# Attention and mixture-of-experts layer on one core: first head's maxima made beside the q and k products, v kept in memory

## The chip, the cores and the metric

The kernel runs on one core of a Trainium2 chip. Its engines are PE (matrix products), DVE, ACT and POOL (element work), SP (here only an issuer of DMAs) and 16 DMA engines. The metric is the time of one execution in device microseconds (us), smaller is better.

## The reference, cut to what matters

Input x has 4 batches of 2048 tokens of 256 values. The layer norm of x goes both to an attention of 16 heads of 16 values and to a mixture of 16 experts; the sum of x and both results is returned.

```python
xn = _layernorm(x)
q = (xn @ Wq.T + bq).reshape(b, s, HEADS, HEAD_DIM) * SCALE      # k, v alike, without the scale
scores = jnp.einsum('bqhd,bkhd->bhqk', q, k)
probs = jax.nn.softmax(scores, axis=-1)
out = jnp.einsum('bhqk,bkhd->bqhd', probs, v).reshape(b, s, d) @ Wo.T + bo
# experts: two of 16 are gated per token, each expert takes its 1024 best tokens of a batch, gelu(x w1) w2, layer norm
```

## The kernel before

The kernel has four stages, each a block of per-engine programs; an engine enters a stage when all engines have left the one before.

**norm** (L157 to L343) goes over 16 blocks of 512 tokens (4 a batch). DVE makes statistics (L226, L230) and normalised tokens (L239), PE transposes them (L320) and multiplies with Wv and the gate's weights (L330), DVE's `take` adds the bias and writes v into `v_all` (L246), 64 KB in each partition that stay on chip. SP loads x two blocks ahead (L198) and stores the normalised tokens (L202). DVE's order is `take` of turn t - 1, `scale` of block t + 2, `statistics` of block t + 3.

**project** (L346 to L484): for each of 16 blocks four products of 128x512 (two halves each of q and k, L385). ACT evacuates each twice (L409, L411), POOL subtracts to get the rounding rest (L424), SP stores both parts, 512 KB a product (L432). One buffer for each of the four: ACT writes part m of a block only when part m of the block before has landed, and PE makes product m of a block only when ACT has written part m of the block before. Beside this DVE makes the experts' routing (L447 to L482); PE waits for it after 4 blocks (L392), transposes the routes, and goes on.

**attend** (L487 to L875) has 64 heads. A head n has a first pass, 32 pairs of products (L771, 48 rows) whose maxima DVE takes (L852); from them the shift is made (ACT L731, POOL L579, DVE's transpose L843) and put by four small DMAs into two rows of q's features (`put_shift`, L653). Then come the scores (L781, 50 rows), their exponentials (ACT L724) and the weighing with v (L790), by key tile of 128. The first pass of the following heads is written between the scores: during head g PE makes the last 22 pairs of head g + 1 and the first 10 (`EARLY`) of head g + 2. Only head 0's 32 pairs and head 1's first 10 stand ahead of all scores (L820 to L825). A `feed` (L641) is four DMAs from `q_parts` and `k_parts`: two of 256 KB, which write 32 rows of 8 KB from a source of shape [2, 16, 2048], and two of 128 KB over 16 rows; each head needs one for the first pass (LOWER) and one for the scores (UPPER). SP issues all of them, in order. POOL copies each head's v from `v_all` to `v_head` (L573), and looks for the experts' bounds.

**finish** makes the experts, the output projection and the sum.

## Time and profile before

| | us |
|---|---|
| median of 3 runs (lowest to highest) | 3443.64 (3443.12 to 3445.09) |
| the profiled execution | 3444.21 |
| its span in the trace | 3442.4 |
| norm stage, from the start to the first product of q and k | 102.2 |
| project stage, to the first feed's issue | 239.4 |
| first passes ahead of the scores, to the first score | 315.8 |
| PE busy over the span | 3296.2 (96%) |
| DVE busy | 2894.2 (84%) |
| ACT busy | 2526.4 (73%) |

Times of instructions are counted from the span's start. A line in a profile row (L771) is the line of the kernel before. "x8" is the number of instructions in a row; "[12.29 <-DVE cand L482]" says that the engine stood 12.29 us before it, until that instruction. PEclk is the clock granted to PE: 1.00 is 2.4 GHz, 0.50 is 1.2 GHz. A DMA share is the mean busy share of the 16 DMA engines.

### The profile page before, as it was taken

The numbers are of one execution on the slowest core, as the hardware profiler recorded it, in microseconds if no ns is written. First come the engines' busy times: TensorE is split into PE (matmuls) and PEld (weight loads), VectorE is DVE, ScalarE is ACT, GpSimd is POOL, SyncE is SP. The second block draws the span as 40 slices with busy tenths as digits, with TensorE's granted clock in tenths as the row PEclk, the third lists the DMA queues.
The fourth block names the chain that finished last, engine by engine and source line by source line (L and its number), as shares of the span: only waits on it lengthen the run. The fifth ranks groups of instructions, "written<-read, shape, count | busy, mean of one in ns | idle before, by whom it ended". The sixth has DMA issues, their size and how long they took to land. (4 is left out here: it accounts for less than half of the span.)

```text
span 3442.4 us, 74610 instructions
## 1 busy us (share of the span) xinstructions
PE 3296.2 (96%) x20848; PEld 1706.4 (50%) x20848; DVE 2894.2 (84%) x2987; ACT 2526.4 (73%) x5726; POOL 929.1 (27%) x1339
## 2 busy tenths in 40 slices
PE   7868999999999999999999999999999999599998
PEld 6424444444444444444444444444444444288887
DVE  7508999999999999999999999999999998267777
ACT  3452888888888888888888888888888888443433
POOL 2550222222222222222222222222222222144443
PEclk9986999999999999999999999999999999799999
DMA  6581111122111211111121111211111121355553
GB/s 198 173 241 33 50 54 54 54 60 59 58 56 55 56 56 55 54 54 54 54 60 56 56 55 54 63 56 56 55 54 54 54 59 47 112 136 169 160 164 117
DMA packets 133063, 272.29 MB, mean 79 GB/s; under 512 B 22512, under 2 KB 68656, under 8 KB 120432
## 3 DMA queue, kind: packets, MB, share of 16 engines
q1 hardware_dynamic: 130464, 266.68, 26.7%
q8 instruction: 176, 2.88, 0.4%
q10 hardware_dynamic: 2256, 1.36, 0.2%
q14 instruction: 167, 1.37, 0.1%
HBM read 173.59 MB, written 84.93 MB: 75 GB/s over the span
## 5 line engine op out<-in xcount | busy, mean ns | idle before, releaser
L852 DVE TENSOR_REDUCE half_max<-m_ps 128x1 f32<-128x1024 f32 x2048 | 2413.4, 1220 | 324.5 <-PE m_ps L771 308.8
L724 ACT ACTIVATE prob<-s_ps 128x512 f32<-128x512 f32 (+1 forms) x5120 | 2188.3, 520 | 425.8 <-PE s_ps L781 423.2
L781 PE MATMUL s_ps<-q_feat,k_feat 50*128 50x512 f32 (+1 forms) x5120 | 1538.0, 396 | 7.5 <-issue 4.7
L771 PE MATMUL m_ps<-k_feat,q_feat 48*128 48x512 f32 x4096 | 1405.1, 448 | 55.9 <-DMA k_feat<-k_parts 28.4
L781 PEld LDWEIGHTS s_ps<-q_feat,k_feat 50*128 50x128 f32 x5120 | 796.2, 184 | 983.3 <-ACT prob L724 870.6
L790 PE MATMUL a_ps<-prob,v_head 128*32 128x512 f32 x8192 | 1091.6, 605 | 0.0
L771 PEld LDWEIGHTS m_ps<-k_feat,q_feat 48*128 48x128 f32 x4096 | 616.3, 187 | 287.5 <-DVE half_max L852 248.6
L579 POOL TENSOR_TENSOR shift<-row_max,shift 128x16 fp32r<-128x16 f32 x64 | 14.2, 222 | 1213.0 <-ACT shift L731 1213.0
L790 PEld LDWEIGHTS a_ps<-prob,v_head 128*32 128x32 f32 x8192 | 161.2, 108 | 253.7 <-issue 211.7
L1134 ACT ACTIVATE g_hi<-g 128x512 fp32r<-128x512 f32 x128 | 81.0, 632 | 243.8 <-DVE g L1172 199.8
L1297 POOL TENSOR_TENSOR g_lo<-g,g_hi 128x512 fp32r<-128x512 f32 x128 | 173.0, 1352 | 229.2 <-ACT g_hi L1134 229.2
L606 POOL TENSOR_SCALAR step_of<-route,cand 64x256 f32<-64x256 f32 x217 | 198.6, 915 | 44.5 <-POOL held L607 38.3
L573 POOL COPY v_head<-v_all 128x256 f32 (+1 forms) x64 | 25.3, 397 | 660.2 <-PE a_ps L790 660.1
L607 POOL TENSOR_TENSOR held<-held,step_of 64x256 f32<-64x256 f32 x217 | 157.6, 726 | 39.8 <-POOL step_of L606 39.8
L1172 DVE TENSOR_TENSOR g<-g,mask_bc 128x512 f32<-128x512 f32 x128 | 133.5, 1043 | 36.0 <-ACT g L1131 30.7
L1067 PE MATMUL o_ps<-w_hi,g_hi 128*128 128x256 f32 x512 | 144.6, 282 | 6.1 <-issue 3.7
L1067 PE MATMUL o_ps<-w_lo,g_hi 128*128 128x256 f32 x512 | 144.3, 282 | 0.0
L1067 PE MATMUL o_ps<-w_hi,g_lo 128*128 128x256 f32 x512 | 143.1, 280 | 0.0
L1056 PE MATMUL h_ps<-xn_hi,w_hi 128*128 128x512 f32 x256 | 105.7, 413 | 32.0 <-DMA b_rows<-b_parts 32.0
L1131 ACT ACTIVATE g<-h_ps,b_col 128x512 f32<-128x512 f32 x128 | 86.2, 674 | 25.7 <-PE h_ps L1056 25.7
L1067 PEld LDWEIGHTS o_ps<-w_hi,g_hi 128*128 128x128 f32 x512 | 96.5, 189 | 12.0 <-issue 7.1
L1056 PE MATMUL h_ps<-xn_lo,w_hi 128*128 128x512 f32 x256 | 102.1, 399 | 0.0
(132 smaller groups left out, 1904.1 us busy)
## 6 DMA issues: line engine op xcount, KB each, us to landing
q_feat<-q_parts SPq DMA_DIRECT2D x128, 256.0 KB
k_feat<-k_parts SPq DMA_DIRECT2D x128, 256.0 KB
q_parts<-parts SPq DMA_DIRECT2D x32, 512.0 KB, 4.8
k_parts<-parts SPq DMA_DIRECT2D x32, 512.0 KB, 4.8
q_feat<-q_parts SPq DMA_DIRECT2D x128, 128.0 KB
k_feat<-k_parts SPq DMA_DIRECT2D x128, 128.0 KB
att_dram<-att SPq DMA_DIRECT2D x64, 256.0 KB, 14.0
mask_bc<-mask_b SPq DMA_DIRECT2D x128, 128.0 KB, 4.4
```

The lines of the kernel that those rows point to most:

```text
L606: do(pool.tensor_scalar(step_of[:, :], t["route"][:, c * PART:(c + 1) * PART], bound, None, ALU.is_ge))
L607: do(pool.tensor_tensor(held[:, :], held[:, :], step_of[:, :], ALU.add))
L724: act.activation(prob[tile(r, kt) % R][:, cols(j)], s_ps[slot(r, kt, j) % R][:, wide(j)], ACT.Exp).then_inc(exped, 1)
L771: ins = pe.matmul(m_ps[p % 2][:, k * BLK:(k + 1) * BLK], q_feat[r % 2][LOW, qt * P:(qt + 1) * P], k_feat[r % 2][LOW, key:key + BLK], start ...
L781: pe.matmul(s_ps[slot(r, kt, j) % R][:, wide(j)], k_feat[r % 2][UP, kt * P:(kt + 1) * P], q_feat[r % 2][UP, cols(j)], start=True, stop=Tru ...
L790: ins = pe.matmul(a_ps[qb * VW:(qb + 1) * VW, :], v_head[r % R][:, kt, :], prob[tile(r, kt) % R][:, qb * BLK:(qb + 1) * BLK], start=(kt == ...
L852: dve.tensor_reduce(half_max[r][:, p // 2, p % 2:p % 2 + 1], m_ps[p % 2][:, :], AX.X, ALU.max).then_inc(maxed, 1)
L1056: ins = pe.matmul(h_ps[e % 2][:, :], w, v, start=(c == 0 and k == 0), stop=(c == KC - 1 and k == 2))
L1067: ins = pe.matmul(o_ps[k], v, w[:, e, :], start=(e == 0 and m == 0), stop=False)
L1131: act.activation(g[e % 2][:, :], h_ps[e % 2][:, :], ACT.Gelu, bias=b1_col[:, e:e + 1]).then_inc(gelu, 1)
L1172: dve.tensor_tensor(g[e % 2][:, :], g[e % 2][:, :], mask_bc[q % 2][:, e % QTR, :], ALU.mult).then_inc(gated, 1)
L1297: pool.tensor_tensor(g_lo[e % 2][:, :], g[e % 2][:, :], g_hi[e % 2][:, :].bitcast(F32), ALU.subtract).then_inc(split, 1)
```

## The change

v goes to memory: `v_all` is replaced by `v_buf`, two batches long, from which SP stores each batch (2.10 MB) in the norm stage; before each block of DVE's `take` stands a wait for the store two batches back. In the attention SP loads each head's v (128 KB) and POOL copies from there. The maxima's tiles, the features and their semaphores are made before the project stage; the two banks of maxima (`m_ps`) also take the transposed routes. In the project stage PE waits for the routing after 6 blocks instead of 4, and of the remaining 40 products each is followed by one pair of first passes, two of them by two: all 32 pairs of head 0 and the first 10 of head 1. SP issues three feeds (heads 0 and 1 for the first pass, head 0 for the scores) once batch 0's parts have landed, behind the fifth block's stores and ahead of the sixth's. The shift of head 0 is made and put at the end of the stage. The ones in the features are written by two POOL memsets at the start instead of POOL and ACT at the start of the attention. The mask's steps get memory of their own instead of `v_all`'s.

The diff, cut to its core:

```diff
+PAIRS = ST * 2
+EARLY = 10
+LOADS = 4
+BEFORE = 6
 HALVES = NBLK * KC
...
 
-            for u in range(2):
-                load(u, u)
-            with sp.Fori(1, NBLK // 2) as i:
-                for u in range(2):
-                    load(i * 2 + u, u)
-                    store(i * 2 + u - 2, u)
-            for u in range(2):
-                store(NBLK - 2 + u, u)
+            def store_v(b):
+                sp.wait_ge(taken, TPB + (b + 1) * ST)
+                sp.dma_start(t["v_dram"][b * H:(b + 1) * H].rearrange("h p f -> p h f"),
+                             v_buf[:, b % 2, :, :, :].rearrange("p h s d -> p h (s d)")).then_inc(v_stored, 16)
+
+            sp.sem_inc(v_stored, 32)
+            for blk in range(2):
+                load(blk, blk)
+            for blk in range(2, NBLK):
+                if blk % BPS == 0 and blk >= 2 * BPS:
+                    store_v(blk // BPS - 2)
+                load(blk, blk % 2)
+                store(blk - 2, blk % 2)
+            store_v(B - 2)
+            for blk in range(NBLK - 2, NBLK):
+                store(blk, blk % 2)
+            store_v(B - 1)
+            sp.wait_ge(v_stored, 32 + 16 * B)
             for u in range(2):
                 sp.wait_ge(xn_stored[u], 16 * (NBLK // 2))
 
...
+                dve.wait_ge(v_stored, (blk // BPS) * 16 + 16)
                 for k in range(TPB):
                     dve.wait_ge(projected, blk * TPB + k + 1 + 2 * TPB)
                     dve.tensor_tensor(
-                        v_view[:, ds(blk // BPS, 1), ds((blk % BPS) * TPB + k, 1), :, :].rearrange("p b s h d -> p (b s h) d"),
+                        v_view[:, ds((blk // BPS) % 2, 1), ds((blk % BPS) * TPB + k, 1), :, :].rearrange("p b s h d -> p (b s h) d"),
                         vg_ps[:, k, 0:D].rearrange("p (h d) -> p h d", h=H),
                         t["bv_bc"][:, :].rearrange("p (h d) -> p h d", h=H), ALU.add).then_inc(taken, 1)
...
+            pool.wait_ge(ident_made, 1)
+            for u in range(2):
+                pool.memset(t["k_feat"][u][96:P, :].bitcast(F32), 1.0).then_inc(cleared, 1)
+                pool.wait_ge(cleared, 3 + u)
...
-            def chunks(lo, hi):
-                with pe.Fori(lo, hi) as blk:
-                    for m in range(M):
-                        pe.wait_ge(rounded, blk * M + m + 1)
-                        for c in range(KC):
-                            half = m % KC
-                            ins = pe.matmul(qk_ps[m][:, :], weights[m][:, c, half * P:(half + 1) * P],
-                                            t["tok_all"][:, ds(blk, 1), c * BLK:(c + 1) * BLK].rearrange("p n s -> p (n s)"),
-                                            start=(c == 0), stop=(c == KC - 1))
-                        ins.then_inc(scored, 1)
-
-            chunks(0, NBLK // 4)
+            def chunk(blk, m):
+                pe.wait_ge(rounded, blk * M + m + 1)
+                for c in range(KC):
+                    half = m % KC
+                    ins = pe.matmul(qk_ps[m][:, :], weights[m][:, c, half * P:(half + 1) * P],
+                                    t["tok_all"][:, ds(blk, 1), c * BLK:(c + 1) * BLK].rearrange("p n s -> p (n s)"),
+                                    start=(c == 0), stop=(c == KC - 1))
+                ins.then_inc(scored, 1)
+
+            def first_pass(n, p):
+                if p == 0:
+                    pe.wait_ge(fed_low[n], 16 * LOADS)
+                pe.wait_ge(maxed, n * PAIRS + p + 1)
+                qt, half = divmod(p, 2)
+                for k in range(2):
+                    key = half * 2 * BLK + k * BLK
+                    ins = pe.matmul(m_ps[p % 2][:, k * BLK:(k + 1) * BLK], q_feat[n][low, qt * P:(qt + 1) * P],
+                                    k_feat[n][low, key:key + BLK], start=True, stop=True)
+                ins.then_inc(piece, 1)
+
+            with pe.Fori(0, BEFORE) as blk:
+                for m in range(M):
+                    chunk(blk, m)
 
             pe.wait_ge(routed, 1)
             for s in range(ST):
-                ins = pe.transpose(route_ps[:, s * P:(s + 1) * P], tmp[:, s * B:(s + 1) * B, :].rearrange("p b e -> p (b e)"),
-                                   t["ident"][:, :])
+                half, at = divmod(s, ST // 2)
+                ins = pe.transpose(m_ps[half][0:B * E, at * P:(at + 1) * P],
+                                   tmp[:, s * B:(s + 1) * B, :].rearrange("p b e -> p (b e)"), t["ident"][:, :])
             ins.then_inc(route_t, 1)
-            chunks(NBLK // 4, NBLK)
+
+            early = PAIRS + EARLY
+            turns = (NBLK - BEFORE) * M
+            for blk in range(BEFORE, NBLK):
+                for m in range(M):
+                    chunk(blk, m)
+                    at = (blk - BEFORE) * M + m
+                    for p in range(at * early // turns, (at + 1) * early // turns):
+                        first_pass(p // PAIRS, p % PAIRS)
...
+            act.wait_ge(row_maxed, 1)
+            act.activation(shift[:, 0, :], row_max[0][:, :], ACT.Copy).then_inc(shift_rounded, 1)
 
...
+            pool.wait_ge(shift_rounded, 1)
+            pool.tensor_tensor(shift[:, 1, :], row_max[0][:, :], shift[:, 0, :].bitcast(F32), ALU.subtract).then_inc(shift_done, 1)
...
-            with sp.Fori(0, NBLK) as blk:
-                for m in range(M):
-                    sp.wait_ge(split, blk * M + m + 1 + M)
-                    store(blk, m)
+            def feed(n, where, done):
+                q, k = (t[w][:, n * HD:(n + 1) * HD, :] for w in ("q_parts", "k_parts"))
+                pair, single = slice(where, where + 2 * HD), slice(where + 2 * HD, where + FEAT)
+                sp.dma_start(q_feat[n][pair, :].bitcast(F32), q).then_inc(done[n], 16)
+                sp.dma_start(k_feat[n][pair, :].bitcast(F32), k[0:1].broadcast_to([2, HD, S])).then_inc(done[n], 16)
+                sp.dma_start(q_feat[n][single, :].bitcast(F32), q[0:1].rearrange("k d s -> (k d) s")).then_inc(done[n], 16)
+                sp.dma_start(k_feat[n][single, :].bitcast(F32), k[1:2].rearrange("k d s -> (k d) s")).then_inc(done[n], 16)
+
+            def stores(lo, hi):
+                with sp.Fori(lo, hi) as blk:
+                    for m in range(M):
+                        sp.wait_ge(split, blk * M + m + 1 + M)
+                        store(blk, m)
+
+            stores(0, BPS + 1)
+            for m in range(M):
+                sp.wait_ge(stored[m], 16 * BPS + 16)
+            for n in range(2):
+                feed(n, LOWER, fed_low)
+            feed(0, UPPER, fed_up)
+            stores(BPS + 1, NBLK)
+            sp.wait_ge(shift_turned, 1)
+            rows = q_feat[0][UPPER + FEAT:UPPER + FEAT + SHIFT, :].bitcast(F32).rearrange("k (q j p) -> k q j p", j=quarters, q=ST)
+            for j in range(quarters):
+                sp.dma_start(rows[:, :, j, :], turned[j * SHIFT * ST:(j + 1) * SHIFT * ST, :]).then_inc(shift_in, 16)
             for m in range(M):
                 sp.wait_ge(stored[m], 16 * NBLK + 16)
 
...
-            do(dve.tensor_copy(t["route"][:, :], route_ps[:, :]))
+            for half in range(2):
+                do(dve.tensor_copy(t["route"][:, half * 2 * BLK:(half + 1) * 2 * BLK], m_ps[half][0:B * E, :]))
+            dve.sem_inc(maxed, 2)
+            for p in range(PAIRS):
+                dve.wait_ge(piece, p + 1)
+                dve.tensor_reduce(half_max[0][:, p // 2, p % 2:p % 2 + 1], m_ps[p % 2][:, :], AX.X, ALU.max).then_inc(maxed, 1)
+            dve.wait_ge(maxed, PAIRS + 2)
+            dve.tensor_reduce(row_max[0][:, :], half_max[0][:, :, :], AX.X, ALU.max, negate=True).then_inc(row_maxed, 1)
+            for p in range(EARLY):
+                dve.wait_ge(piece, PAIRS + p + 1)
+                dve.tensor_reduce(half_max[1][:, p // 2, p % 2:p % 2 + 1], m_ps[p % 2][:, :], AX.X, ALU.max).then_inc(maxed, 1)
+            dve.wait_ge(shift_done, 1)
+            dve.transpose(turned[:, :], shift[:, :, :].rearrange("p k q -> p (k q)").bitcast(F32)).then_inc(shift_turned, 1)
 
...
-            def copy_v(n, r):
-                pool.tensor_copy(v_head[r][:, :, 0:HD],
-                                 t["v_all"][:, :, :, :, :].rearrange("p b h s d -> p (b h) s d")[:, ds(n, 1)].rearrange("p n s d -> p (n s) d")
-                                 ).then_inc(v_ready, 1)
+            pool.wait_ge(ones_set, R)
+
+            def copy_v(r, turn):
+                wait_apart(pool, v_loaded[r], (turn + 1) * 16, t["passed"][2])
+                pool.tensor_copy(v_head[r][:, :, 0:HD], v_in[r][:, :, :]).then_inc(v_ready, 1)
...
+            def load_v(n, r):
+                sp.dma_start(v_in[r % R][:, :, :].rearrange("p s d -> p (s d)"),
+                             t["v_dram"][ds(n, 1)].rearrange("n p f -> (n p) f")).then_inc(v_loaded[r % R], 16)
+
             sp.sem_inc(att_out, 16)
             sp.sem_inc(prepared_out, 16)
-            for n in range(2):
-                feed(n, n, LOWER, fed_low)
+            for n in range(R):
+                load_v(n, n)
+            sp.wait_ge(piece, PAIRS)
+            feed(2, 0, LOWER, fed_low)
             for dst, src in ((shift_bc[:, :], "beta"), (staged[:, 0:D].bitcast(F32), "bo")):
                 sp.dma_start(dst, t[src].partition_broadcast(P)).then_inc(bias_in, 16)
-            sp.wait_ge(ones_made, 2)
-            feed(0, 0, UPPER, fed_up)
...
                 if following:
                     put_shift(g + 1, (r + 1) % 2)
                 if third:
+                    sp.wait_ge(v_ready, g + 1)
+                    load_v(g + 3, r)
...
-            for p in range(PAIRS):
-                for k in range(2):
-                    pass1(0, 0, 0, p, k)
-            for p in range(EARLY):
-                for k in range(2):
-                    pass1(1, 0, 1, p, k)
```

## Rows read from the trace of the kernel before

**Rows 1.** Busy us by stretch: span, then PE, PEld, DVE, ACT, POOL; PEclk, DMA share, GB/s.

```profile
20.00:100.00 80.00, 73.45 (x361) 59.59 (x360) 64.84 (x237) 28.91 (x56) 16.40 (x26) 1.00 0.51 174
...
142.00:148.00 6.00, 5.78 (x19) 3.88 (x20) 2.23 (x3) 0.00 (x0) 0.00 (x0) 0.50 0.00 0
...
152.00:232.00 80.00, 77.52 (x181) 34.01 (x179) 0.00 (x0) 58.21 (x91) 58.00 (x46) 1.00 1.00 293
...
260.00:300.00 40.00, 36.77 (x63) 15.87 (x64) 37.31 (x34) 0.21 (x1) 0.72 (x1) 0.50 0.08 28
```

**Rows 2.** Timeline of PE and of SP's queue, 225 to 316: start, us, what.

```profile
225.92 3.60 PE L385 MATMUL qk_ps<-tok_all,wkT_sb 128*128 x8
...
239.36 0.84 SPq L644 DMA_DIRECT2D q_feat<-q_parts  x1
...
257.87 2.07 PE L771 MATMUL m_ps<-k_feat,q_feat 48*128 48x512 f32 x4 [28.35 <-DMA k_feat<-k_parts]
...
298.25 0.65 SPq L644 DMA_DIRECT2D q_feat<-q_parts  x1
...
301.09 3.97 SPq L653 DMA_DIRECT2D q_feat<-turned  x4
...
315.78 0.76 PE L781 MATMUL s_ps<-q_feat,k_feat 50*128 50x512 f32 x1 [4.75 <-issue]
```

**Rows 3.** Groups of instructions, 0 to 340: DVE's reduces (busy, mean ns | idle).

```profile
L852 DVE TENSOR_REDUCE half_max<-m_ps 128x1 f32<-128x1024 f32 x59 | 70.0, 1220 | 122.0 <-PE m_ps L771 121.6
```

**Rows 4.** Timeline of PE in the attention: the weighing products, one key tile apart.

```profile
338.88 1.06 PE L790 MATMUL a_ps<-prob,v_head 128*32 128x512 f32 x8
...
341.42 1.07 PE L790 MATMUL a_ps<-prob,v_head 128*32 128x512 f32 x8
```

**Rows 5.** DMA queues, 3425 to 3443: GB/s in slices of 0.45 us; issue and landing.

```profile
GB/s 0 18 0 0 0 0 36 0 0 0 0 0 0 0 0 0 0 18 0 0 0 0 0 0 0 0 0 0 0 0 0 0 0 280 344 348 194 0 0 0
...
out<-res SPq DMA_DIRECT2D x1, 512.0 KB, 2.9
```

**Rows 6.** DMA queues, 152 to 230, the products stage: packets.

```profile
DMA packets 11917, 22.99 MB, mean 295 GB/s; under 512 B 695, under 2 KB 695, under 8 KB 11917
```

**Rows 7.** Timeline of DVE and SP, 40 to 48, the norm stage.

```profile
40.35 0.21 DVE L250 TENSOR_TENSOR logits<-vg_ps,bg_bc 128x64 f32 x1
...
42.26 0.38 SPq L198 DMA_DIRECT2D x_in<-in_x  x1
...
47.41 1.40 DVE L226 BATCH_NORM_STATS2 bn<-x_in 128x6 f32<-128x256 f32 x4
```

**Rows 8.** DMA issues of the whole run: KB each, median us to landing.

```profile
x_in<-in_x SPq DMA_DIRECT2D x16, 512.0 KB, 4.0
...
tok_hi_dram<-staged SPq DMA_DIRECT2D x32, 256.0 KB, 13.0
```

**Rows 9.** Timeline of PE at the start of the products stage.

```profile
102.20 3.69 PE L385 MATMUL qk_ps<-tok_all,wqT_sb 128*128 x8 [1.27 <-ACTq L401]
...
119.47 3.60 PE L385 MATMUL qk_ps<-tok_all,wkT_sb 128*128 x8
...
122.90 3.60 PE L385 MATMUL qk_ps<-tok_all,wqT_sb 128*128 x8
```

**Rows 10.** Timeline, 121 to 146: POOL, SP's queue and PE around the routing.

```profile
121.45 15.45 POOL L424 TENSOR_TENSOR parts<-f32s,parts 128x512 fp32r<-128x512 f32 x8 [0.26 <-ACT parts L411]
...
134.72 2.58 SPq L432 DMA_DIRECT2D k_parts<-parts  x2
...
142.22 3.62 PE L394 MATMUL route_ps<-ident,work 128*64 128x128 f32 x16 [12.29 <-DVE cand L482]
```

**Rows 11.** DMA queues, 250 to 254, 266 to 270, 278 to 282 (tenths, 0.1 us each).

```profile
DMA packets 28, 0.21 MB, mean 53 GB/s; under 512 B 2, under 2 KB 2, under 8 KB 2
...
DMA packets 60, 0.18 MB, mean 45 GB/s; under 512 B 10, under 2 KB 42, under 8 KB 42
...
DMA  0300300300400400000000000000000000000000
```

101 lines of the change are left out of this document (49 added, 52 removed).

## The prediction

> **What bounds the kernel now.** I read the page's forty slices first: PE is busy in nearly all of them, except the start and one slice before the last stage. Of the start I then read the table by stretch [rows 1]. The norm stage keeps PE and DVE near full (73 and 65 of 80 us). In the products stage PE and the DMA engines are both full: from 152 to 232 PE is busy 77.5 of 80 and the DMA share is 1.00, at 293 GB/s. Between the stages PE stands: 229.5 to 257.9 [rows 2], 28.4 us, while stores land and the first feeds travel. Then come 32 pairs of first passes for head 0 and 10 for head 1, paced by DVE's reduce (1.22 us each [rows 3], with its wait 1.27: 41 and 13 us), with the clock at 0.50 and only DVE and PE at work [rows 1]. The first score starts at 315.8 [rows 2]. From there each key tile takes 2.55 us of PE without a break [rows 4], up to the end of the attention. So what the change is worth is read from one number: **when the first score starts**. All that is saved or lost before it moves the end one to one, if the steady state is untouched.
>
> The sum is made against the profiled run, 3444.2 us (span 3442.4), which lies 0.6 us above the median of 3443.6.
>
> **Part 1, v through memory: what the norm stage pays.** Removed: nothing, since `take` still writes the same tile of the same size. Added: four stores of 2.10 MB each, in pieces of 1 KB. The nearest row is the output store at the kernel's end, also 1 KB pieces: 344 GB/s in its burst and 2.9 us to landing for 0.5 MB [rows 5]. I take 300 GB/s, so 7.0 us a store. Bounds: 6.1 us at 344 GB/s; and 13.4 us, if each of 2048 packets costs an engine what a packet of the products stage does (16 engines x 78 us / 11917 = 0.105 us, and 128 packets an engine) [rows 6].
> - Two of the stores stand in SP's queue ahead of the loads of blocks 8 and 12. The store may start once DVE has taken the batch's last tile (40.6), the load is issued at 42.3 and its statistics start at 47.4 [rows 7]. The load lands a median 4.0 us after issue [rows 8], so it has 1.1 us to spare. With some 0.9 us from issue to the first byte, the store's data move from about 41.4 to 48.4, where the load's began at 43.2: 5.2 us later, less 1.1 of slack, less 0.7 of waits that DVE regains: 3.4 us, twice, 7 us. Lower bound 0, if the load overtakes; upper 10 each, with the slow store. Behind DVE stand PE and ACT, which have no second source of work.
> - The third store is behind nothing that is waited for. The fourth is issued after the very last `take` (about 101.5), and the stage's end waits for it; before, PE stood only 1.3 us between the stages [rows 9]. Issue 0.4, data 7.0, landing 1.6: **9 us** (8 to 16).
> Together +16 us (+8 to +36). The DMA page of the Trainium skill (DMA: Bandwidth & Descriptors, Anatomy of one DMA) fits a transfer as about 2.0 us plus bytes at 436 GB/s, for a store 6.8 us from issue to landing where I use 9; by it this part would be some +10. The bursts of the output store stay below that rate, so my own number stands. POOL's two memsets run while the first x load travels (4.0 us from issue to landing [rows 8]) and are priced at nothing; at 1.3 us each, a POOL operation of 128x512 [rows 1], they would cost at most 3 us if that cover were gone. The copies of v into v_head are as many and as large as before.
>
> **Part 2, products up to the feeds.** Before, PE stood 12.3 us for `routed`, up to 142.2, and nothing was stored then [rows 10]. With 6 blocks ahead of that wait instead of 4 the wait is gone; this is worth up to 12 us and is inside the sum below. PE starts at half clock after about 10 us of standing, as it did at 142 [rows 1]; I add 1.5 us. The fourth block's last store was issued at about 137.3; while DVE's routing chain runs, POOL takes 15.45 us for 8 subtractions, so a block takes 7.7 [rows 10]. The fifth block is stored at 145, and with parts 1 and 2 the feeds are issued at 145 + 16 + 1.5 = **162.5**.
>
> **Part 3, the feeds inside the products.** Twelve DMAs, three feeds. Before, they were issued from 239.4; PE had the first at 257.9, after 18.5 us [rows 2], and the last of them moved at 279.5 [rows 11], 40 us after the first issue. In between the rate was 53 GB/s, in packets of 8 KB [rows 11], where 16 engines moved 293 and were full [rows 1]. I read this as two engines at 26 GB/s each. These are the 256 KB DMAs, whose source has an outermost size of 2. The other engines stood; 32 packets of 512 B to 2 KB, left of the two bias loads that were issued behind the first two feeds, moved only at 266 to 270 [rows 11], and in the attention, where feeds are always about, a 256 KB store takes 13 us to land [rows 8]. So the order on those two engines is kept, and whatever is issued later waits for them. A split of parts needs all 16 engines, so block 5's stores land only when the three feeds have drained: 40.1 us, less 4 for the two bias loads that now come later (an estimate, 32 packets in the stretch 266 to 270), plus 1.5 of stores still ahead, 37.6; plus 1.8 (0.5 MB at 293 GB/s) and 1.6 to landing: 41 us after issue, **203.5**. ACT cannot write block 6's parts before that (a landed store is its wait), and PE's product (7, 0) waits for ACT. Before it, PE has only block 6 and the passes 0 to 3 between, which need the first feed at about 182. So PE mostly stands from 164 to 204.5.
> The Trainium skill (same page, Rules for kernel authors) says that an outermost size c below 16 confines a DMA to at most c engines. The trace agrees. Its specification of some 27 GiB/s an engine would drain 1.57 MB over two engines in 27 us rather than 36; the sum would come out 9 us lower by it. I keep the measured drain.
>
> **Part 4, products and passes to the end.** From 204.5: 36 products at 1.72 us (8 records in 3.43 us from start to start, four records a product [rows 9]) make 62; 38 pairs of passes at 0.43 us make 16 (at half clock four passes run 0.43 us apart [rows 2], so 0.21 at full). PE is thus the slower side at 8.6 us a block, against 7.2 for the stores. Half clock after the stall costs 3.2 us, as after 142 (some 6.4 us at 0.50) [rows 1]. End of the last product: about 285. DVE has 42 reduces of 1.22 us, 51 us, beside 80: hidden. Without that cover they would be the 54 us that stand there now.
> Then 1.3 us ACT (two operations, 58.2 us for 91 [rows 1]), 1.3 POOL (58.0 for 46), 0.5 for shift and transpose (an estimate, tiles of 128x32), 4.0 for four put DMAs [rows 2], 1.6 to landing: first score at **293.7**. The 10 us that it waited before for these puts, which stood behind the third feed's pair DMAs (issued at 298.2, puts to 305.1, score 315.8 [rows 2]), are gone, since that feed now comes later. The first weighing needs v in SBUF two key tiles later, 5 us at least, and three 128 KB loads come first in SP's queue: hidden. Its cover is only these 5 us; a late load would show there.
>
> **Sum.** 315.8 - 293.7 = 22 us earlier. 3444.2 - 22 = **3422 us**. What moves it: v stores 8 less or 20 more (that end is a rival below), the drain by 5 either way. Its own range is 3408 to 3437.
>
> **Part 5, the steady state.** Each head gains one SP issue (about 0.4 us) and one wait that is long met; it stands before a feed that has a whole head (41 us) of time. POOL's copy gets a wait on a load issued a head earlier. I price both at nothing; covers are those 41 us. The mask's steps get their own memory, which changes no instruction.
>
> **Rivals.**
> - *The feeds hold up less* (chance 0.18). If stores overtake the feeds on the two engines, these still carry 37.6 us of feeds plus 11 blocks at 7.2, from 162.5: 279. First score not before 285, gain 31, 3413. If other engines take a share, PE alone bounds: 163 + 69 + 18 + 2 + 8 = 260, gain 55, 3389. For it: the share is low only while nothing else is in the queue. Against: the bias packets.
> - *v stores run at the packet price of the products stage* (0.12): part 1 is 36 instead of 16; 3442, no change. For it: pieces are 1 KB and strided by 128 KB. Against: the output store.
> - *The clock stays low* (0.08), the rival on the other side. Place: products and passes after the stall. Price: at 1.2 GHz 78 us of PE work become 156, 3501, slower. It decides from 42 us spent at half clock. For it: from 260 to 300 PE was busy 92% and the clock stayed at 0.50 [rows 1], with these same 48-row passes. Against: the transposes and products after 142 brought it back in 6.4 us. By the Trainium skill (TensorE: Matmul & The Clock Gate, Part 1) sustained activity releases the throttle, which would leave my forecast as it is; rows 260 to 300 show that these passes alone did not.
> - *A small loss in each head* (0.08) from the extra load before the feed: 0.3 us x 64 = 19 us gives 3442, 0.5 us gives 3455. Nothing in the rows shows SP or DMA late there.
> - *The change does not do what it says*, passes only after the products: excluded by the written order, but a stall of `maxed` or of feed 1 would look like it; it is inside the forecast's range.
>
> **Numbers.** Forecast 0.54. A measurement of this kernel can tell 0.2%, 7 us, so faster means below 3437. Faster: 0.50 of the forecast, 0.18, 0.02 of the rest: 0.70. Same: 0.04 + 0.08 + 0.04 = 0.16. Slower: 0.04 + 0.08 + 0.02 = 0.14. Range 3393 to 3448: from near the first rival's far end to beyond the slow stores.
>
> **What would show it.** DVE standing before the statistics of blocks 8 and 12, some 3 us each; a 10 us gap before the first product; no gap before the route's transposes; a stretch of some 40 us in the products stage with 53 GB/s while ACT waits for a stored part; PE then busy to about 285; the first score near 294; 2.55 us a key tile as before. Wrong would be: a full DMA share through the feeds, a clock of 0.50 late in the stage, or a head longer than before.

## The result, and the profile after

The changed kernel takes **3462.3 us** (median of 5 runs, 3460.1 to 3465.7) where the kernel before takes 3444.0 beside it (5 runs, 3443.1 to 3445.1): a ratio of 1.0054, 95% interval 1.0040 to 1.0069. It is 18 us slower, outside the range of the forecast. The profiled execution took 3464.7, its span is 3462.9; before it was 3444.2 and 3442.4.

| stage mark, us from the start | before | forecast | after |
|---|---|---|---|
| first product of q and k | 102.2 | 118 | 120.5 |
| first feed issued | 239.4 | 162.5 | 162.7 |
| product (7, 0) | | 204.5 | 205.0 |
| end of the last product of q and k | 229.5 | 285 | 299.4 |
| first score | 315.8 | 293.7 | 306.7 |
| last transpose of a shift | 2910.7 | 2888.7 | 2908.6 |
| last output of a head taken | 2961.3 | 2939.3 | 2978.4 |
| first h_ps product of the last stage | 2993.3 | 2971.3 | 3007.5 |
| end of the span | 3442.4 | 3420.4 | 3462.9 |

(The last four marks of the forecast are those of before, less 22.) First the page of after, the engines' busy time and the granted clock in 40 slices:

```profile
PE 3326.3 (96%) x20848; PEld 1710.0 (49%) x20848; DVE 2900.9 (84%) x2988; ACT 2525.8 (73%) x5724; POOL 933.5 (27%) x1340
PEclk9988999999999999999999999999999999699999
```

and of the page of before its clock:

```profile
PEclk9986999999999999999999999999999999799999
```

PE is busy 30 us longer with as many instructions. One digit of the clock near the start is higher than before (8 for 6), one near the end lower (6 for 7), so the clock is no worse at the start, and what it costs must lie late. The timeline of PE, norm and products stage of after [rows 2, 9 for before]:

```profile
120.47 2.07 PE L424 MATMUL qk_ps<-tok_all,wqT_sb 128*128 x2 [9.45 <-ACTq L462]
...
181.60 1.22 PE L436 MATMUL m_ps<-k_feat,q_feat 48*128 48x512 f32 x2 [13.08 <-DMA k_feat<-k_parts]
...
204.96 3.78 PE L424 MATMUL qk_ps<-tok_all,wqT_sb 128*128 128x512 f32 x4 [10.11 <-ACT parts L472]
...
216.49 0.73 PE L436 MATMUL m_ps<-k_feat,q_feat 48*128 48x512 f32 x2
217.15 1.98 PE L424 MATMUL qk_ps<-tok_all,wqT_sb 128*128 128x512 f32 x4
219.06 0.73 PE L436 MATMUL m_ps<-k_feat,q_feat 48*128 48x512 f32 x2
219.72 1.98 PE L424 MATMUL qk_ps<-tok_all,wqT_sb 128*128 128x512 f32 x4
...
297.40 1.98 PE L424 MATMUL qk_ps<-tok_all,wkT_sb 128*128 128x512 f32 x4
...
306.71 0.76 PE L862 MATMUL s_ps<-q_feat,k_feat 50*128 50x512 f32 x1 [6.18 <-DMA q_feat<-turned]
```

Up to product (7, 0) all came as forecast: 9.45 us of waiting at the stage's end, the first pass at 181.6, the hold until 205. ACT's longest wait there is for a stored part:

```profile
ACT parts L472 <- DMA q_parts<-parts: 35.6, 2, 35.0
```

(us in total, times, longest). Then one turn, a product and a pair of passes, takes 2.57 us (217.15 to 219.72) where I had 1.72 + 0.43 = 2.15. So the first score comes 9.1 us earlier than before, not 22. The rest was lost later, where I had put nothing. ACT in the last head, after, and PE at the pause:

```profile
2924.09 1.64 ACT L806 ACTIVATE prob<-s_ps 128x256 f32<-128x256 f32 x4 [0.42 <-PE s_ps L862]
2927.21 2.82 ACT L806 ACTIVATE prob<-s_ps 128x512 f32<-128x512 f32 x6 [1.49 <-PE s_ps L862]
2930.87 2.35 ACT L806 ACTIVATE prob<-s_ps 128x256 f32<-128x256 f32 x5 [0.84 <-PE s_ps L862]
2934.94 2.35 ACT L806 ACTIVATE prob<-s_ps 128x256 f32<-128x256 f32 x5 [1.71 <-PE s_ps L862]
...
2978.39 0.60 ACT L818 ACTIVATE att<-a_ps 128x512 f32<-128x512 f32 x1 [2.13 <-PE a_ps L871]
```

```profile
2927.86 1.04 PE L862 MATMUL s_ps<-q_feat,k_feat 50*128 50x512 f32 x3 [1.15 <-ACT prob L806]
```

and the table by stretch of the same time, after and then before (columns: stretch, length, busy us of PE, its weight loads, DVE, ACT and POOL with counts; granted clock, DMA share, GB/s):

```profile
2905.00:2920.00 15.00, 14.24 (x82) 5.53 (x78) 11.48 (x10) 12.56 (x32) 7.50 (x4) 1.00 0.06 20
2930.00:2950.00 20.00, 20.00 (x69) 7.35 (x65) 0.00 (x0) 11.59 (x26) 0.00 (x0) 0.50 0.08 20
2955.00:2960.00 5.00, 5.00 (x17) 2.06 (x16) 0.00 (x0) 2.97 (x7) 0.00 (x0) 0.50 0.00 0
```

```profile
2930.00:2950.00 20.00, 19.02 (x104) 7.35 (x104) 0.00 (x0) 16.65 (x40) 1.28 (x1) 1.00 0.10 28
2955.00:2960.00 5.00, 4.88 (x33) 1.68 (x32) 0.00 (x0) 4.16 (x10) 0.00 (x0) 1.00 0.00 0
```

There is a pause of 1.49 us on ACT (on PE 1.15) in the last head, and behind it the clock is 0.50 from 2929.3 to 2977.1, nearly to the end of the attention: a key tile takes 4.07 us instead of 2.55 (2934.94 less 2930.87), since PE is now the slower side at 100% busy. From the last transpose of a shift to the last output it is 69.8 us after and 50.6 before: **19.2 us lost in one head**.

The 42.5 us between the forecast's end (3420.4) and the span's are thus: 13.0 at the first score, 7.9 in the first heads, 1.0 gained in the heads behind them, 19.2 in the last head, 2.9 gained up to the first h_ps product, 6.3 in the last stage (455.4 us instead of 449.1). The 7.9 are 4.9 up to the third transpose of a shift (at 390.3, only 4.2 us ahead of before's 394.5) and 3.0 up to the next (434.4 against 435.6), while the clock was 0.50 from 386.4 to 396.7; at the fifth after is 1.1 us ahead (475.6, before 476.7), at the last 2.1.

In the first heads and in the last stage two stalls of DVE are new. After:

```profile
382.06 0.19 DVE L927 TENSOR_REDUCE row_max<-half_max 128x16 f32<-128x32 f32 x1
383.60 3.49 DVE L925 TENSOR_REDUCE half_max<-m_ps 128x1 f32<-128x1024 f32 x3 [1.36 <-PE m_ps L852]
...
3043.72 0.74 DVE L1250 TENSOR_TENSOR z<-z,o_ps 128x256 f32<-128x256 f32 x2
3049.80 0.75 DVE L1250 TENSOR_TENSOR z<-z,o_ps 128x256 f32<-128x256 f32 x2 [5.34 <-issue]
```

The first is named a wait for PE, but PE itself stood 1.57 us there for DVE; the second lies between two of four equal additions, and PE, whose products they take, stood 3.2 us there for DVE too. Before, the first gap is 0.24 us and the four additions run through:

```profile
388.43 1.23 DVE L852 TENSOR_REDUCE half_max<-m_ps 128x1 f32<-128x1024 f32 x1 [0.24 <-issue]
...
3029.60 1.40 DVE L1178 TENSOR_TENSOR z<-z,o_ps 128x256 f32<-128x256 f32 x4
```

A third new pause is ACT's, nine times, once a turn of its loop over six heads, some 6.5 us behind a transpose and 0.8 to 1.1 us long; a head with it takes 41.5 to 41.8 us instead of 41.1. One of the nine:

```profile
1390.75 1.57 ACT L806 ACTIVATE prob<-s_ps 128x512 f32<-128x512 f32 x3 [1.02 <-PE s_ps L862]
```

### The profile page after: what moved, and what is told of

Same layout as the page of the kernel before. It is cut to its first block and busy times, and to the rows that moved or that the text cites. A ratio compares the mean times of both kernels' runs of the same rounds, so it can differ in the third digit from the quotient of the medians.

```text
span 3462.9 us, 74796 instructions
## 1 busy us (share of the span) xinstructions
PE 3326.3 (96%) x20848; PEld 1710.0 (49%) x20848; DVE 2900.9 (84%) x2988; ACT 2525.8 (73%) x5724; POOL 933.5 (27%) x1340
## 3 DMA queue, kind: packets, MB, share of 16 engines
q10 hardware_dynamic: 2256, 1.36, 0.2%
## 5 line engine op out<-in xcount | busy, mean ns | idle before, releaser
L925 DVE TENSOR_REDUCE half_max<-m_ps 128x1 f32<-128x1024 f32 x2006 | 2363.4, 1220 | 218.2 <-PE m_ps L852 209.3
L852 PE MATMUL m_ps<-k_feat,q_feat 48*128 48x512 f32 x4012 | 1357.7, 443 | 18.4 <-DVE half_max L925 18.2
L871 PE MATMUL a_ps<-prob,v_head 128*32 128x512 f32 x8192 | 1105.9, 612 | 0.0
L852 PEld LDWEIGHTS m_ps<-k_feat,q_feat 48*128 48x128 f32 x4012 | 598.5, 186 | 218.2 <-DVE half_max L925 208.8
L871 PEld LDWEIGHTS a_ps<-prob,v_head 128*32 128x32 f32 x8192 | 162.0, 108 | 262.5 <-issue 213.9
L658 POOL COPY v_head<-v_in 128x256 f32<-128x256 f32 x64 | 25.5, 398 | 676.5 <-PE a_ps L871 675.1
L487 POOL TENSOR_TENSOR parts<-f32s,parts 128x512 fp32r<-128x512 f32 x64 | 89.1, 1401 | 92.5 <-ACT parts L472 92.4
```

The source lines that it names most:

```text
L487: pool.tensor_tensor(parts[m][:, 1, :], f32s[m][:, :], parts[m][:, 0, :].bitcast(F32), ALU.subtract).then_inc(split, 1)
L852: ins = pe.matmul(m_ps[p % 2][:, k * BLK:(k + 1) * BLK], q_feat[r % 2][LOW, qt * P:(qt + 1) * P], k_feat[r % 2][LOW, key:key + BLK], start ...
L871: ins = pe.matmul(a_ps[qb * VW:(qb + 1) * VW, :], v_head[r % R][:, kt, :], prob[tile(r, kt) % R][:, qb * BLK:(qb + 1) * BLK], start=(kt == ...
L925: dve.tensor_reduce(half_max[r][:, p // 2, p % 2:p % 2 + 1], m_ps[p % 2][:, :], AX.X, ALU.max).then_inc(maxed, 1)
```

## The experiments

Two theories of the late losses went into them. **A:** the pauses are an engine's waits for its own next instructions, at fixed places of its code, which the change has moved; a pause lets the clock fall, and in the last head, without first passes between, it stays low. **The rivals:** the v loads or later transfers cost it; or it is chance of timing. For the early loss: changing between products and passes costs PE 0.43 us a turn, or the passes are dearer there. Ratios are to the kernel before, run beside each (3444.1 to 3445.2).

**e1, passes up to the end.** Edit, in PE's `step` of the attention (`idle_pass` is one product of head 63's first pass into `m_ps`, whose result nobody reads; only the first of them waits, for the last maxima):

```diff
+                    if isinstance(g, int) and g >= HEADS - 2 and (g == HEADS - 1 or kt >= 12):
+                        return lambda j: idle_pass(g, r, kt, k, j)
```

> The changed kernel, with first passes whose results nobody reads added to the end of head 62 and to head 63, where it has none (their output is left unread, the result is unchanged). Theory A (the clock): the 19 us that the last head loses come from one pause of 1.2 to 1.5 us at 2927, after which the clock falls to 0.50 and PE, with scores and weighing alone, never gets it back. In heads 0 to 2, where passes stand between, it came back after such a pause within some 13 us. Then the clock returns here too, the attention ends near 2965 instead of 2978, and the whole takes 3447 to 3453. Rival B (work per key tile): the clock stays at 0.50 whatever PE does; a key tile with four passes more then takes 5.1 us instead of 4.07, twelve of them some 12 us more, 3470 to 3478. Rival C: the pause itself comes from a late transfer or an engine and goes or stays by chance; then nothing is added in a key tile (2.55 us) and the pause is seen at another place or not at all, 3444 to 3462.

Measured 3446.0 (3441.6 to 3450.4, 10 runs; ratio 1.0004, 0.9995 to 1.0014), 16 us less than the changed kernel. ACT in the last head:

```profile
2928.20 2.82 ACT L806 ACTIVATE prob<-s_ps 128x512 f32<-128x512 f32 x6 [1.98 <-PE s_ps L870]
2932.61 1.31 ACT L806 ACTIVATE prob<-s_ps 128x256 f32<-128x256 f32 x3 [1.58 <-PE s_ps L870]
...
2936.56 2.13 ACT L806 ACTIVATE prob<-s_ps 128x256 f32<-128x256 f32 x5 [1.36 <-PE s_ps L870]
...
2964.33 0.60 ACT L818 ACTIVATE att<-a_ps 128x512 f32<-128x512 f32 x1 [1.58 <-PE a_ps L879]
```

The pause is in the same place and no shorter; the clock is back at 2936.3, after 6.9 us at 0.50, where 47.8 us of scores and weighing had not brought it back. The last output comes at 2964.3 instead of 2978.4, and the last head takes 55.2 us, before 50.6. So the pause costs little and the clock behind it much. The Trainium skill (TensorE: Matmul & The Clock Gate, What's actually happening) has sustained activity release the throttle; the changed kernel's last head does not agree, busy 20.00 of 20 us at 0.50, and a caveat of the same page (Seeing it yourself), that the gate has been seen stuck for over 50 us, at K = 1/4 where here it is 0.50, comes nearer.

**e2, passes by twos.**

```diff
-                    for p in range(at * early // turns, (at + 1) * early // turns):
-                        first_pass(p // PAIRS, p % PAIRS)
+                    if at % 2 == 1:
+                        for p in range((at - 1) * early // turns, (at + 1) * early // turns):
+                            first_pass(p // PAIRS, p % PAIRS)
```

> The changed kernel with two pairs of first passes after every second product of q and k, instead of one after each: as many products and passes, half the changes from one kind to the other. Theory A (a change from product to pass and back costs PE about 0.43 us, since the first matmul after it starts together with its weight load): the 19 changes saved are worth 8 us, the last product starts near 289 instead of 297.4, the first score near 298.5 instead of 306.7. Rival B (the passes themselves are dearer beside products, through the DMA share or the 48 rows): nothing changes, 297 and 307. Rival C (passes in twos wait for DVE's reduces of 1.22 us, two buffers): the last product is later, by up to 19 x 1.2 us. The whole: 3454, 3462 or up to 3480, if the last head's fall of the clock stays as it is; without that fall 19 less each.

Measured 3455.1 (3432.8 to 3459.8, 10 runs; ratio 1.0029, 1.0014 to 1.0044); one run stands alone at 3432.8, the others lie within 3452 to 3460. The record has the mean granted clock of each run: 0.985 in that one, 0.974 to 0.977 in the others. At 3450 us, 0.008 more is some 55 us fewer at 0.50 (an estimate from these numbers), about the length of the fall in the last head. So the same code most likely ran once without the fall; that run has no trace. PE in the products stage:

```profile
216.19 3.70 PE L424 MATMUL qk_ps<-tok_all,wqT_sb 128*128 128x512 f32 x8
219.82 1.19 PE L436 MATMUL m_ps<-k_feat,q_feat 48*128 48x512 f32 x4
220.94 3.70 PE L424 MATMUL qk_ps<-tok_all,wkT_sb 128*128 128x512 f32 x8
```

Two turns take 4.75 us instead of 5.15: one change to passes and back costs 0.40 us. The last product ends at 292.8 instead of 299.4, the first score comes at 301.2. This is theory A, at 6.6 us at the last product and 5.5 at the first score instead of its 8. In the changed kernel the weight load of each first product or pass behind a change starts together with it:

```profile
216.49 0.29 PEld L436 LDWEIGHTS m_ps<-k_feat,q_feat 48*128 48x128 f32 x2 [0.76 <-DVE half_max L575]
217.15 0.30 PEld L424 LDWEIGHTS qk_ps<-tok_all,wqT_sb 128*128 128x128 f32 x2 [0.36 <-issue]
```

where inside a group it is hidden. The Trainium skill (TensorE: Matmul & The Clock Gate, Step-by-step: what each phase is for) has loads pulled ahead only if their row groups don't conflict or they go to the background buffer; that these 128 and 48 rows share row groups agrees, but no run here separates the two conditions.

**e3, v alone.** The kernel before with only the v parts of the change (stores in the norm stage, `load_v`, `copy_v`).

> The kernel before with v through memory alone; the first head's passes stay where they were. Theory A: the norm stage is 18 us longer (the first product of q and k at 120 instead of 102), all after it shifts by 18 and the steady state is as before: first score at 334, 3462. If the fall of the clock in the last head comes with the v loads or the added instructions of the heads, 19 more, 3481. Rival B (a small loss in each head through the v load): 3462 plus 0.1 to 0.3 us x 64, spread over the heads. Rival C (v costs little, and the passes moved into the products lose the time): 3444 to 3450.

Measured 3460.8 (ratio 1.0052, 1.0035 to 1.0068). The first product of q and k comes at 118.3, the first score at 332.5, 16.8 later than before; theory A of this run. No loss per head: from the first score to the last transpose of a shift it takes 2590.0 us, before 2595.0. And the last head has no pause and no fall of the clock (50.6 us), so the v loads alone do not cause them. DVE's early stall is there, at the same reduce (1.37 us at 406.2), but the clock does not fall behind it, and up to the fifth transpose it costs 1.0 us, not 7.9. The last stage has the stall of DVE here too, 5.72 us between the same additions, and takes 453.9 us.

**e4, ScalarE's instructions moved.**

```diff
         def _(act):
+            for _ in range(40):
+                act.sem_inc(padding, 1)
             act.sem_inc(exped, R)
```

> The changed kernel with 40 semaphore increments that nobody waits for, ahead of the attention's work on ScalarE: the same work, its instructions at other addresses. Theory A (the pauses of 1.2 to 1.6 us at 384.9 and 2927 are ScalarE waiting for its next instructions, at fixed places in the code): the pauses move to other key tiles or become smaller; if the one in the last head shrinks below about 0.5 us the clock does not fall there and the whole takes 3442 to 3446; if it moves within the head, the loss is 1.5 us for each key tile left behind it. Rival B (the pauses come from the data: a late maximum, a transfer): both stay in the same key tiles, 3462. The padding itself costs 1 to 3 us once, hidden behind PE's wait for the shift.

Measured **3438.9** (3436.8 to 3442.1, 10 runs; ratio 0.9985, 0.9975 to 0.9994): 23 us less than the changed kernel, for 40 instructions that do nothing, and below the kernel before. PE's start, ACT's last output, and the table by stretch:

```profile
309.47 0.76 PE L865 MATMUL s_ps<-q_feat,k_feat 50*128 50x512 f32 x1 [8.91 <-ACTq L802]
2953.49 0.60 ACT L821 ACTIVATE att<-a_ps 128x512 f32<-128x512 f32 x1 [1.34 <-PE a_ps L874]
```

```profile
2930.00:2950.00 20.00, 18.98 (x104) 7.32 (x96) 0.00 (x0) 16.63 (x41) 0.00 (x0) 1.00 0.00 1
```

The pause is gone and the clock is full; from the last transpose (2902.8) to the last output 50.6 us, as before the change. The padding itself delays the first score by 2.8 us. The gain is larger than theory A's, since ACT's pauses in the loop, which I had not seen, are gone too: from the fifth transpose to the last 2428.7 us, in the changed kernel 2433.0. And half of theory A failed: the early stall has not moved. It is DVE's, at the same reduce as in the changed kernel and as long,

```profile
384.27 1.23 DVE L928 TENSOR_REDUCE half_max<-m_ps 128x1 f32<-128x1024 f32 x1 [1.36 <-PE m_ps L855]
```

and the pauses that I had put down to ACT, PE's up to 385.6 and ACT's up to 386.4 here, follow from it.

**e7, the control:** the same 40 increments in the kernel before.

> The kernel before with the 40 idle semaphore increments on ScalarE: the control for e4_act_pad. Theory A (pauses of ScalarE at fixed places in its instructions): before has none over 0.4 us in the last head, so most places are harmless and nothing changes, 3441 to 3447; but if the shift puts one in the last head, the clock falls there and it takes 3450 to 3465. Rival B (the padding makes any kernel faster, through something else): 3436 to 3440.

Measured 3445.0 (10 runs; ratio 1.0002, 0.9993 to 1.0012): nothing, as theory A has it. Padding is no gain in itself; nor does it delay the first score here (313.6, before 315.8).

**e9, VectorE's instructions moved as well** (e4 with 40 increments at the head of DVE's part of the attention).

> The padded changed kernel of e4_act_pad with 40 more idle semaphore increments, on VectorE, ahead of its work in the attention. Theory A (the two stalls of VectorE that the changed kernels have and before has not, 1.4 us before the maxima at 384 and 5 to 6 us between two of four equal additions in the last stage, both with nothing that the profile shows as awaited, are waits for its next instructions at fixed places in the code): at least one of them moves or shrinks; if both go, the pause at 384 costs 2 to 4 us less and the last stage 5 us less, 3430 to 3434; if they move to places of the same kind, 3436 to 3445. Rival B (they come from the data, a late transfer or maximum): both stay where they are, 3439 to 3441.

Measured 3434.1 (3432.4 to 3436.4, 7 runs; ratio 0.9972, 0.9961 to 0.9984), 4.7 less than e4. Both stalls are gone:

```profile
381.63 0.19 DVE L934 TENSOR_REDUCE row_max<-half_max 128x16 f32<-128x32 f32 x1
382.05 3.49 DVE L932 TENSOR_REDUCE half_max<-m_ps 128x1 f32<-128x1024 f32 x3 [0.23 <-issue]
...
3016.39 1.40 DVE L1257 TENSOR_TENSOR z<-z,o_ps 128x256 f32<-128x256 f32 x4
```

though the first score stands where e4 has it (309.7). The early stall is thus tied to a place in DVE's code: in all nine kernels that have the v parts and no padding on DVE (the changed one, e1 to e5, e8, e10, e12) it lies ahead of the same reduce, 1.36 or 1.37 us long, at times from 347 (e12) to 405 (e3), and in e9 and e11 it is absent. What it costs depends on the clock: in e2 and e3, where the clock stayed full behind it, the heads up to the fifth transpose take 161.9 and 162.0 us, before 160.9, e9 161.1, and the changed kernel, where it fell, 168.9. The last stage takes 453.5 us, 4.4 more than before; a new stall of DVE of 2.33 us ends at 2987.5, and PE stands 7.08 us there, where it stands 3.66 before. Counted from the last output, e9 needs 481.2 us to the end, before 481.1 and the changed kernel 484.5.

**e5, the pair DMAs split,** on e4:

```diff
-                sp.dma_start(q_feat[n][pair, :].bitcast(F32), q).then_inc(done[n], 16)
-                sp.dma_start(k_feat[n][pair, :].bitcast(F32), k[0:1].broadcast_to([2, HD, S])).then_inc(done[n], 16)
+                for c in range(2):
+                    part = slice(where + c * HD, where + (c + 1) * HD)
+                    sp.dma_start(q_feat[n][part, :].bitcast(F32), q[c:c + 1].rearrange("k d s -> (k d) s")).then_inc(done[n], 16)
+                    sp.dma_start(k_feat[n][part, :].bitcast(F32), k[0:1].rearrange("k d s -> (k d) s")).then_inc(done[n], 16)
```

> The padded changed kernel of e4_act_pad with each 256 KB pair DMA of a feed split into two of 128 KB whose rows all lie in the outermost dimension, everywhere (18 DMAs for the three feeds in the products, 24 in a head's place of 16). Theory A (the stores of parts of block 5 wait 35 us because the pair DMAs run on two engines at 53 GB/s and keep their order there): the stretch at 53 GB/s goes, product (7, 0) starts near 173 instead of 205, the last product near 266, the first score near 278 instead of 309.5; the whole 3407 to 3411. Rival B (the stores wait for the feeds' bytes or packets as such, not for two engines): the hold stays above 20 us, 3425 or more. Rival C (more DMA issues on SP cost the heads time): 0.3 us x 64 = 19 us given back, 3428.

Measured 3426.1 (ratio 0.9942, 0.9925 to 0.9959), 12.7 less than e4, between the theories. The stretch at a quarter share is gone:

```profile
172.00:182.00 10.00, 5.62 (x8) 2.17 (x8) 1.22 (x1) 0.00 (x0) 0.60 (x1) 0.51 1.01 159
```

(share 1.01 at 159 GB/s where after had 0.25 at 82), ACT's longest wait for a stored part is 13.7 us instead of 35.0, the first score comes at 290.0, 19.5 earlier than e4. I had expected 31: the first pass, in PE's order ahead of products (6, 1) to (6, 3), still waits for its feed until 176.4, and (7, 0) starts at 187.3, not 173. So two engines explain most of the hold; the feeds' own bytes are the likely rest. Some 5 us are given back in the attention, 3.3 of them up to the fifth transpose, where the clock is 0.50 for 6.8 us (e4: 3.4); that is far from rival C's 19.

**e6, the same split in the kernel before.**

> The kernel before with the same split of the pair DMAs and nothing else. Theory A: the first pass starts near 246 instead of 257.9, since a feed no longer takes 18 us; the puts of the shift no longer stand behind a third feed on two engines, 4 to 8 us; the passes stay paced by DVE's reduces at 1.27 us: first score near 298 instead of 315.8, 3426 to 3430. Rival B (the wait of 28 us is for the last stores, not for the feeds): 3440 to 3444. Rival C (more issues cost the heads time): 3445 or more.

Measured 3430.7 (ratio 0.9959, 0.9945 to 0.9974). First pass at 246.7 instead of 257.9, first score at 299.2 instead of 315.8: theory A. This one edit gains 14 us without the change.

**e8, v stores out of the way,** on e4:

```diff
-                if blk % BPS == 0 and blk >= 2 * BPS:
-                    store_v(blk // BPS - 2)
                 load(blk, blk % 2)
+                if blk % BPS == 0 and blk >= 2 * BPS:
+                    store_v(blk // BPS - 2)
...
-            sp.wait_ge(v_stored, 32 + 16 * B)
```

(`v_buf` is kept over the products stage, and the wait stands at that stage's end.)

> The padded changed kernel with the v stores out of the way in the norm stage: the loads of blocks 8 and 12 are issued ahead of the v stores that share SP's queue, and the tile of v is kept until the end of the products stage, so that the norm stage does not wait for the last v store. Theory A (3.4 us at each of the two loads and 9 us at the stage's end): the first product of q and k starts near 104 to 107 instead of 120.4, and all after it is as much earlier, 3423 to 3427. Rival B (the v stores slow all loads and stores of the stage by their bytes, wherever they stand): 5 to 9 us of the 18 stay, 3428 to 3433.

Measured 3430.9 (ratio 0.9962, 0.9948 to 0.9976), 8 less than e4. PE's gap between the stages is 1.77 us instead of 9.4:

```profile
110.71 1.55 PE L425 MATMUL qk_ps<-tok_all,wqT_sb 128*128 x3 [1.77 <-ACTq L463]
```

So 9.7 us of the 18 were the end wait (7.7) and the order of two loads (2.0); the other 8.5 stay in this order too (rival B), spread over the norm stage: the load issued behind a v store now lands 7.3 and 7.6 us after its issue instead of 4.

**e10, e11, e12, the parts together.** e10 is e4 with e2, e5 and e8; e11 has DVE's padding too; e12 has e2, e5, e8 and e1's passes, and no padding.

> The parts that the runs showed to cost, mended together: ScalarE padded, v stores behind the loads and not waited for at the end of the norm stage, pair DMAs split in two, first passes in twos. If the gains add up: from 3438.9, less 8 to 10 (v), 13 to 19 (split), 6 to 8 (twos): 3402 to 3412. If the products stage becomes bound by its stores (7.2 us a block, DMA share 1.00), the passes in twos are worth nothing: 3409 to 3420. If a pause of an engine meets the end of the attention, 10 to 20 more.

> e10_combined with 40 idle increments on VectorE as well. Theory A (stalls at fixed places in VectorE's code): the same difference to e10_combined as e9_pad_dve has to e4_act_pad, and in the same places of the code. Rival B (stalls set by time and traffic): the difference is another one, or none.

> e10_combined without any idle increments, and with the unread first passes in the last head of e1_passes_to_end: does the gain rest on where the instructions happen to lie? Theory A (the pause of ScalarE in the third key tile of the last head comes back with the old addresses, whatever the time, and the passes bring the clock back in some 10 us): the pause is there again, about 6 us behind VectorE's last head change; it costs 5 to 9 us and the padding's own 2.8 us are saved: 3408 to 3414. Rival B (the pause depended on the time at which the attention started, which is now 30 us earlier): no pause there, 3402 to 3405. Rival C (the passes alone do not bring the clock back): 3422 to 3427.

| | median us (runs) | ratio to before | first score | last output |
|---|---|---|---|---|
| e10 | 3406.3 (4) | 0.9891 (0.9874 to 0.9907) | 276.7 | 2920.2 |
| e11 | 3405.0 (4) | 0.9889 (0.9873 to 0.9906) | 275.2 | 2916.6 |
| e12 | 3424.6 (4) | 0.9947 (0.9931 to 0.9964) | 275.2 | 2933.7 |

The gains add up, and e10 beats the kernel before by 38 us. e11 is not to be told from e10 by its time; in its trace the early stall (e10: 1.36 us at 350.4) and the one between the additions are gone as in e9. e12 missed theory A's range; it lies in rival C's, but not by rival C's mechanism: its pause in the last head is in the old place of the code,

```profile
2900.33 2.82 ACT L813 ACTIVATE prob<-s_ps 128x512 f32<-128x512 f32 x6 [1.28 <-PE s_ps L877]
```

27 us earlier than in the changed kernel, so it does not go by the time; the clock does not fall there, and the last head costs 51.8 us. But ACT's pause in each turn of the loop over six heads, which e10 has not, is back at its old place and is now 1.4 to 1.8 us long, and twice, at 1850 and at 2600, the clock falls behind it. I had not expected that, though the changed kernel, e1 and e2 have the pause too (0.8 to 1.3 us); why it is longer here is open. Between the first score and the last transpose e12 takes 2606.7 us and e10 2592.8.

## Why the prediction was wrong

- **Part 1, v through memory: right in size** (+16 forecast, +18.3 in the changed kernel; e3 has +16.1 at the first product and +16.8 at the first score), half right in its split. At the stage's end PE stands 9.45 us where it stood 1.27, 8.2 more (forecast 9). DVE stands 2.9 and 3.1 us ahead of blocks 8 and 12 (forecast 3.4 each), but the stage is 10.1 us longer, not 7, and e8 shows that most of it does not come from these two loads. The fit that the prediction sets beside its own number (the Trainium skill, DMA: Bandwidth & Descriptors, Anatomy of one DMA; 6.8 us a store) is given there for DMAs that GpSimd issues, and these are issued by SP: the four took 7.5 to 8.3 us from issue to landing, my 9 was too high.
- **Parts 2 and 3, feeds inside the products: right in time.** Feeds at 162.7, (7, 0) at 205.0. That two engines cause the hold is shown by e5 and e6 for most of it. One detail came otherwise: SP needed 18 us to issue the twelve DMAs, so the store behind them was issued at 180.7, not at once, and landed at 204.2 (forecast 203.5).
- **Part 4 failed first, in the size of one term.** "38 pairs of passes at 0.43 us", 16 us, is the price of passes among passes; each turn pays another 0.42 for the change from 128 rows to 48 and back (2.57 us instead of 2.15, e2). Over some 35 turns behind (7, 0) that is 15 us; the last product ended 14.4 later than forecast, the first score came 13.0 later, for the tail between them was 1.4 us shorter than I had it. I had rows of passes alone and of products alone, and none of the two in turn.
- **Part 5 failed by more, and not in size alone.** It priced the attention at nothing, from engines and queues in its middle. There it was right: the heads behind the fifth transpose take 1.0 us less than before in all. The loss lies at the edges: 7.9 in the first heads, 19.2 in the last, 6.3 in the last stage. What the runs show in its place: the change moves code, an engine pauses for 1.4 to 1.5 us at a fixed place of it, and where the clock falls behind the pause, the clock costs far more than the pause. For ACT in the last head e4 (moved: 50.6 us instead of 69.8), e12 (same place, 27 us earlier in time) and e1 (clock back, 55.2 us) show it; for DVE in the first heads e9 does (161.1 us up to the fifth transpose instead of 168.9). Of the last stage's 6.3, the stall of 5.3 us (PE stood 3.2 for it) goes with DVE's padding in e9 and e11, and in e9 a smaller one comes; counted from the last output, e9 loses nothing against before.
- **The rivals.** "The clock stays low" named the right mechanism in the wrong stage; a "small loss in each head" is excluded by e3.

With the pauses moved away (e9) the change gives 3434, 10 us faster than before, ratio 0.9972. That is not half of the forecast come true. In e9 the first score comes 6.1 us earlier than before, not 22: 13.0 are lost in Part 4 and some 3 to the padding. Another 5.7 us come from the heads, 2589.3 us from the first score to the last transpose instead of 2595.0, for which the prediction had nothing; e3 has them too (2590.0), so they go with the v parts, and why is open. Without the pauses moved away the change is 18 us slower. What it "is worth" differs by 28 us with the place of 80 instructions that do nothing.

That these pauses are loads of instructions is argued, not shown. For it: in the four kernels with the pause in the last head (the changed one, e1, e2, e12) a packet of 8 KB on an instruction queue starts 0.0 to 0.3 us ahead of it (2925.71 in the changed kernel, ACT standing from 2925.72 to 2927.21), and another 0.7 to 0.9 us behind its end (2927.88); in e4 that queue moves nothing between 2916 and 2950. Against a simple reading: before has four such packets between 2924.9 and 2934.5 and no pause of ACT over 0.42 us in its last head, and at DVE's early stall the only one starts 0.4 us behind its end. The Trainium skill (Advanced Engine Details and Errata, ISA Cache) gives an engine two lines of 256 instructions; a pause at fixed places of unrolled code that 40 instructions shift would agree. No run here varied the amount of padding, which would show the period.

## What to carry to other kernels

Price a turn of mixed work from rows of the mixture: two kinds of product that each run well alone cost PE 0.4 us for every change there and back, so group them. Where only scores and weighing follow, one pause of 1.5 us at the start can cost the whole stretch its clock (here 19 us in one head); look at the last iteration apart from the steady state, and compare a structural change only after moving its code by some tens of idle instructions, in both kernels. A DMA whose outermost size is 2 not only is slow itself, it holds up what is issued behind it (ACT waited 35.0 us for such a store, 13.7 with the DMAs split).

## What the runs showed of the hardware

- At a granted clock of 0.50, PE busy 20.00 of 20 us did not bring it back in 47.8 us of scores and weighing; with four passes of 48 rows more in a key tile it was back after 6.9 (e1).
- The length of a pause does not tell whether the clock falls. In the last head a pause of PE of 1.15 us (the changed kernel), 1.41 (e1) and 1.45 (e2) was followed by the fall, one of 0.71 (e12) was not. But in e12's loop the fall came behind pauses of 0.87 and 0.68 us and not behind one of 0.79, and a pause of 1.6 us in the first heads (e2, e3, e10, e12) and one of 1.92 at 2798.8 (e10) were not followed by it.
- 40 semaphore increments on ScalarE delay the first score of the changed kernel by 2.8 us and change the total by -23, in the kernel before by 0 (e7); e12 and e10, which differ by them and by e1's passes, lie 18 us apart.
- Three feeds in rows of 8 KB kept the DMA share at 1.01 while moving 159 GB/s (e5), where the stores of parts moved 293 at the same share [rows 1].
